# Attention spreads as turned columns, and the four layer norms moved from ScalarE to GpSimd

## The reference

```
h = relu(layernorm(x)); x = x + gat0(h, adj)     # one head:  Wh = h W^T; e = leaky(s1_i + s2_j); masked softmax; att @ Wh
h = relu(layernorm(x)); x = x + gat1(h, adj)     # four heads of 32 columns: the same with a bias, mask adj == 1
h = relu(layernorm(x)); x = x + sess(h, adj)     # sigmoid of leaky(h a_k h^T), chosen by adj == 1..4, times h, plus bias
h = relu(layernorm(x)); x = x + ggnn(h, adj)     # 3 GRU layers: m = A^T (h w); gi = m W_ih^T; gh = h W_hh^T; gates
```

## Time and profile before

| | |
|---|---|
| median of three runs | 1065.93 us (1064.18 to 1067.51) |
| the profiled execution's own time | 1066.04 us |
| its span, first to last instruction | 1063.9 us |
| granted TensorE clock, mean | 0.967 |
| PE (TensorE matmul) busy | 954.6 us, 90% |
| DVE (VectorE) busy | 892.3 us, 84% |
| ACT (ScalarE) busy | 864.0 us, 81% |
| POOL (GpSimd) busy | 132.6 us, 12% |

### The profile page before, as it was taken

One profiled execution on the slowest core, in us unless ns is written; L12 is line 12 of the kernel. 1 busy time (PEld: TensorE's weight loads), 2 busy tenths in 40 slices (PEclk: granted clock), 3 DMA queues, 4 the chain that ended last, 5 costly groups with the idle time before them and its releaser, 6 DMA issues.

```text
span 1063.9 us, 16086 instructions
## 1 busy us (share of the span) xinstructions
PE 954.6 (90%) x5024; PEld 609.6 (57%) x5024; DVE 892.3 (84%) x2710; ACT 864.0 (81%) x1860; POOL 132.6 (12%) x170
## 2 busy tenths in 40 slices
PE   4588998999989899999989899998989999998866
PEld 3455565666566566656556566656656665655443
DVE  5296989899898979899897989989897989979543
ACT  3367888979888897988888897988889798887742
POOL 1102011010202011020201201020201101010000
PEclk8558999999999999999999999999999999999989
DMA  2401204021210403121220402121030302111000
GB/s 72 109 1 39 72 11 109 11 61 52 68 51 14 106 11 77 44 60 51 56 64 10 110 11 60 60 61 51 15 105 11 79 31 61 50 40 51 1 11 10
DMA packets 42477, 52.32 MB, mean 49 GB/s; under 512 B 1296, under 2 KB 25872, under 8 KB 42384
## 3 DMA queue, kind: packets, MB, share of 16 engines
q0 software_dynamic: 16896, 25.17, 10.7%
q1 hardware_dynamic: 17040, 21.83, 6.5%
q10 hardware_dynamic: 8448, 4.20, 1.3%
HBM read 55.39 MB, written 4.19 MB: 56 GB/s over the span
## 4 chain that ended last, share of the span: by engine, by line
PE 52%; DVE 28%; ACT 10%; issue 6%; POOL 3%; DMA 0%; DVEq 0%; SPq 0%; ACTq 0%; POOLq 0%
PE l_bank L948 7%; DVE probs L642 6%; PE a_bank L981 6%; PE x_bank L1040 4%; PE a_bank L948 3%; PE h_bank L1102 3%; ACT hn L394 3%; PE r_bank L1102 3%; PE r_bank L1105 3%; DVE sess L843 3%; DVE sess L836 3%; PE h_bank L1105 3%; PE n_bank L1105 3%; DVE probs L663 3%; POOL rstd L363 2%
## 5 line engine op out<-in xcount | busy, mean ns | idle before, releaser
L663 DVE SCALAR_TENSOR_TENSOR probs<-spread,s_lift,probs 128x512 f32<-128x512 f32 x320 | 237.4, 747 | 4.0 <-DVE rmax L642 0.5
L642 DVE CUSTOM_DVE_ANT_0 probs<-spread,mask 128x512 f32<-128x512 f32 x320 | 211.8, 684 | 2.4 <-ACT spread L450 2.3
L363 POOL TENSOR_TENSOR rstd<-var_eps,power 128x4 f32<-128x4 f32 x64 | 88.0, 1375 | 882.5 <-DVE var_eps L636 603.0
L460 ACT ACTIVATE probs<-probs,shift_p 128x512 f32<-128x512 f32 x256 | 185.7, 725 | 5.7 <-DVE shift_p L659 5.7
L468 ACT ACTIVATE pT<-l_bank 128x512 f32<-128x512 f32 x256 | 151.8, 600 | 46.5 <-PE l_bank L948 46.3
L948 PEld LDWEIGHTS l_bank<-ident,probs 128*128 128x128 f32 x1024 | 124.3, 144 | 73.8 <-issue 46.0
L948 PE MATMUL l_bank<-ident,probs 128*128 128x128 f32 x1024 | 150.5, 278 | 6.1 <-ACT probs L460 5.1
L394 ACT ACTIVATE hn<-x,shift,rstd 128x128 f32<-128x128 f32 x192 | 80.5, 492 | 26.1 <-POOL shift L365 26.0
L1005 PE MATMUL l_bank<-hT,dst_rep 128*128 128x512 f32 x128 | 73.6, 658 | 12.1 <-ACT pT L468 8.5
L870 DVE SCALAR_TENSOR_TENSOR hid_n<-r_t,hid_n 128x512 f32<-128x512 f32 x48 | 33.1, 689 | 57.8 <-ACT r_t L518 57.8
L981 PE MATMUL a_bank<-values,pT 128*128 128x128 f32 x512 | 65.7, 286 | 0.7 <-ACT pT L428 0.7
(11 more groups left out here) (175 smaller groups left out, 1956.5 us busy)
## 6 DMA issues: line engine op xcount, KB each, us to landing
adjt_i<-in_adj_t SPq DMA_DIRECT2D x16, 1024.0 KB, 5.2
edges<-in_adj POOLq DMA_DIRECT2D x16, 1024.0 KB, 5.9
adj_h<-in_adj POOLq DMA_DIRECT2D x16, 512.0 KB, 7.7
xin<-in_x SPq DMA_DIRECT2D x16, 256.0 KB, 2.9
out<-out_sb ACTq DMA_DIRECT2D x16, 256.0 KB, 3.8
weights_sb<-in_weights SPq DMA_DIRECT2D x1, 840.0 KB, 4.7
```

What stands on the lines that cost most here:

```text
L363: g.tensor_tensor(rstd[n][:], var_eps[n][:], power[:], op=ALU.pow).then_inc(pool_step[n], 1)
L460: s.activation(row, row, ACT.Exp, bias=shift_p[:, head, c:c + 1], accum_out=den[:, head, c:c + 1]).then_inc(probs_ready, 1)
L642: return v.tensor_tensor_reduce(out=row, in0=spread_row, in1=mask, scale=1.0 / LIFT, scalar=-3e38, op0=ALU.subtract, op1=ALU.max, accum_ou ...
L663: v.scalar_tensor_tensor(row, spread_row, source, row, ALU.min, ALU.subtract, reverse1=True).then_inc(ready, 1)
```

## The change

Its parts, all in one step:

1. **Spreads.** `dst_rep` goes. The weights of the values get the source and target vectors as further columns (`values0_w` 130 wide, `values1_w` 136 wide), so one product of `hT` gives values, source and target numbers as columns. The spread of a head is then made by four transposes of its target column, read with a step of zero over 128 columns (`spread_column`), into the same bank. gat0's values no longer fit a bank, so three chunks go first and the last in a step of its own (`last0`), each with a ScalarE copy. `src0`, `s1_lift` and VectorE's L682 and L741 go; the two adds of gat1's values are 272 columns wide and take the constants along.
2. **Norms.** VectorE's minus the mean (L634) and GpSimd's multiply (L365) go. GpSimd makes `hn` without the ramp, four `tensor_scalar` of 128x128, (x - mean) times rstd. The ramp is taken by the copies that follow: `hT` by Relu in place of Copy, `state_hi` by Relu, `state_lo` by max(hn, 0) - state_hi. `hTa` is now read from `hT` instead of the bank, behind a wait for the copy of `hT`. For norm 2 the product with the rows needs the ramp too, so GpSimd takes it in place in one instruction of 128x512 behind TensorE's transposes (`ramp2`), and TensorE's w0 waits for it (`ramp_done`).
3. **Waits.** `turn_rows` waits for each chunk of `hn` instead of all four.
4. **Order.** New keys. In the steady part: values0 and last0 stand before dst0; values1 before x2, and x2 before g1_turn, on TensorE; values1 before scaled on VectorE; stats0, aggr0 and mean0 before g1_joint_r on VectorE. Between g0_agg and x2 (the next graph's) TensorE has the steps it had, less g1_turn and with values1; between scaled and mean3 VectorE has those it had, less values1 and src0. GpSimd: mean1 norm1_0..3 mean0 norm0_0..3 mean2 norm2_0..3 ramp2 edges values1 mean3 norm3_0..3.

```diff
+            def norm(p, n, c, rows):
+                if c == 0:
+                    pool.wait_ge(pool_step[n], p.count(1, 1))
+                    if p.before().exists():
+                        pool.wait_ge(hT_ready[n], p.before().count(1, 1))
+                g.tensor_scalar(hn[n][:, c, :], rows[:, c, :], moments[n][:, c, 0:1], rstd[n][:, c:c + 1],
+                                op0=ALU.subtract, op1=ALU.mult).then_inc(hn_ready[n], 1)
...
+                if step == "ramp2":
+                    pool.wait_ge(hT_ready[2], p.count(1, 1))
+                    g.tensor_scalar(hn[2][:, :, :], hn[2][:, :, :], 0.0, None, op0=ALU.max).then_inc(ramp_done, 1)
...
-                s.activation(hn[n][:, c, :], rows[:, c, :], ACT.Relu, bias=shift[n][:, c:c + 1],
-                             scale=rstd[n][:, c:c + 1]).then_inc(hn_ready[n], 1)
...
-                s.activation(hT[n][:, :], src[:, :], ACT.Copy).then_inc(hT_copied[n], 1)
+                s.activation(hT[n][:, :], src[:, :], ACT.Relu).then_inc(hT_copied[n], 1)
...
-                    s.activation(hTa[:, :], x_bank[:, :], ACT.Identity,
+                    act.wait_ge(hT_copied[2], p.count(1, 1))
+                    s.activation(hTa[:, :], hT[2][:, :], ACT.Identity,
...
-                v.tensor_scalar(minus_mean[n][:, :], moments[n][:, :, 0], -1.0, None, ALU.mult)
...
-                    for half in range(2):
-                        both = l_banks[half][:, 0:2 * (D + H1)].rearrange("p (c k) -> p c k", c=2)
-                        pair = slice(2 * half, 2 * half + 2)
-                        v.tensor_tensor(values1[:, pair, :], both[:, :, 0:D],
-                                        b1_rows[:, :].unsqueeze(1).to_broadcast([P, 2, D]), ALU.add)
-                        last = v.scalar_tensor_tensor(s1_lift[:, 1:HEADS, pair],
...
+                        both = l_banks[half][:, 0:2 * COLS1].rearrange("p (c k) -> p c k", c=2)
+                        v.tensor_tensor(values1[:, 2 * half:2 * half + 2, :], both,
+                                        b1_rows[:, :].unsqueeze(1).to_broadcast([P, 2, COLS1]),
+                                        ALU.add).then_inc(val1_copied, 1)
...
+            def spread_column(dst, columns, k, ready):
                 for c in range(C):
+                    last = t.transpose(dst[:, c * P:(c + 1) * P], columns[:, c, k:k + 1].to_broadcast([P, P]), ident[:])
+                last.then_inc(ready, 1)
...
+                    for c in range(C - 1):
+                        last = t.matmul(a_bank[:, c * COLS0:(c + 1) * COLS0], hT[0][:, c * P:(c + 1) * P],
+                                        values0_w[:, :], start=True, stop=True)
+                    last.then_inc(val0_ready, 1)
+                elif step == "last0":
+                    pe.wait_ge(val0_copied, p.count(1, 1))
+                    t.matmul(a_bank[:, 0:COLS0], hT[0][:, (C - 1) * P:], values0_w[:, :], start=True,
+                             stop=True).then_inc(last0_ready, 1)
...
-                    t.matmul(a_bank[:, :], dst_rep[:, 0, :], hT[0][:, :], start=True, stop=True).then_inc(dst0_ready, 1)
+                    pe.wait_ge(last0_copied, p.count(1, 1))
+                    spread_column(a_bank, values0, D + 1, dst0_ready)
...
-                    t.matmul(l_banks[head % 2][:, :], dst_rep[:, head, :], hT[1][:, :], start=True,
-                             stop=True).then_inc(dst_ready, 1)
+                    spread_column(l_banks[head % 2], values1, TARGET1 + head - 1, dst_ready)
...
+                        pe.wait_ge(ramp_done, p.count(1, 1))
```

More of the change, by code:

```diff
@@ L20 @@
 PLAIN = 1024.0
-A_STEPS = (["stats0", "aggr0", "mean0"] + [f"norm0_{c}" for c in range(4)] + ["rows0", "mask0", "dst0", "src0", "values0"] + [f"m{c}" for c in range(4)]
+A_STEPS = (["stats0", "aggr0", "mean0"] + [f"norm0_{c}" for c in range(4)] + ["rows0", "mask0", "values0", "last0", "dst0"] + [f"m{c}" for c in range(4)]
            + ["u0", "top0", "u1", "t0", "below0", "u2", "t1", "max0", "u3", "t2", "t3", "den0", "rden0"] + [f"sum0_{c}" for c in range(4)] + ["x1"])
-L_STEPS = (["stats1", "aggr1", "mean1"] + [f"norm1_{c}" for c in range(4)] + ["count", "rows1", "mask1", "dst1", "edges", "values1"]
+L_STEPS = (["stats1", "aggr1", "mean1"] + [f"norm1_{c}" for c in range(4)] + ["count", "rows1", "mask1", "edges", "values1", "dst1"]
            + [f"n{c}" for c in range(4)] + ["dst2"]
@@ L31 @@
 B_STEPS = ([f"sum1_{j}" for j in range(4)] + ["den1", "scaled", "x2", "stats2", "aggr2", "mean2"]
-           + [f"norm2_{c}" for c in range(4)] + ["rows2"] + [f"z{n}" for n in range(4)] + ["kinds"]
+           + [f"norm2_{c}" for c in range(4)] + ["rows2", "ramp2"] + [f"z{n}" for n in range(4)] + ["kinds"]
            + [f"s{n}" for n in range(4)] + [f"w{n}" for n in range(4)] + ["x3", "stats3", "aggr3", "mean3"]
@@ L280, in graph_layers @@
         pool_step = [sem(f"pool_step{n}") for n in range(NORMS)]
-        ln_ready = [sem(f"ln_ready{n}") for n in range(NORMS)]
         hn_ready = [sem(f"hn_ready{n}") for n in range(NORMS)]
@@ L381, in step_of @@
                     deviation(p, int(step[4]))
+                if step[:5] == "norm0":
+                    norm(p, 0, int(step[6]), xin[:, p.graph % 2, :, :])
+                if step[:5] == "norm1":
+                    norm(p, 1, int(step[6]), x1[:, p.graph % 2, :, :])
+                if step[:5] == "norm2":
+                    if step == "norm2_0" and p.before().exists():
+                        pool.wait_ge(av2_done, p.before().count(1, 1))
+                    norm(p, 2, int(step[6]), x2)
+                if step == "ramp2":
+                    pool.wait_ge(hT_ready[2], p.count(1, 1))
+                    g.tensor_scalar(hn[2][:, :, :], hn[2][:, :, :], 0.0, None, op0=ALU.max).then_inc(ramp_done, 1)
+                if step[:5] == "norm3":
+                    if step == "norm3_0" and p.before().exists():
+                        pool.wait_ge(rest_ready, p.before().count(LAYERS, 1))
+                    norm(p, 3, int(step[6]), x3)
             load_adj(Place(0))
@@ L389, in _ @@
             s = nc.scalar
-            def norm(p, n, c, rows):
-                if c == 0:
-                    act.wait_ge(ln_ready[n], p.count(1, 1))
-                s.activation(hn[n][:, c, :], rows[:, c, :], ACT.Relu, bias=shift[n][:, c:c + 1],
-                             scale=rstd[n][:, c:c + 1]).then_inc(hn_ready[n], 1)
             def copy_hT(p, n, src):
                 act.wait_ge(hT_ready[n], p.count(1, 1))
-                s.activation(hT[n][:, :], src[:, :], ACT.Copy).then_inc(hT_copied[n], 1)
+                s.activation(hT[n][:, :], src[:, :], ACT.Relu).then_inc(hT_copied[n], 1)
             def step_a(p, step):
                 prev = p.before()
-                if step[:5] == "norm0":
-                    norm(p, 0, int(step[6]), xin[:, p.graph % 2, :, :])
-                elif step == "rows0":
+                if step == "rows0":
                     copy_hT(p, 0, a_bank)
@@ L432, in step_l @@
                 prev = p.before()
-                if step[:5] == "norm1":
-                    norm(p, 1, int(step[6]), x1[:, p.graph % 2, :, :])
-                elif step == "rows1":
+                if step == "rows1":
                     copy_hT(p, 1, l_bank0)
@@ L476, in step_b @@
                     s.activation(avT[:, :], x_bank[:, :], ACT.Copy).then_inc(avT_copied, 1)
-                elif step[:5] == "norm2":
-                    if step == "norm2_0" and prev.exists():
-                        act.wait_ge(av2_done, prev.count(1, 1))
-                    norm(p, 2, int(step[6]), x2)
                 elif step == "rows2":
                     copy_hT(p, 2, x_bank)
-                    s.activation(hTa[:, :], x_bank[:, :], ACT.Identity,
+                    act.wait_ge(hT_copied[2], p.count(1, 1))
+                    s.activation(hTa[:, :], hT[2][:, :], ACT.Identity,
                                  scale=sess_sb[:, 0:1]).then_inc(hTa_ready, 1)
@@ L492, in step_b @@
                     s.activation(sess[:, j, :], sess[:, j, :], ACT.Tanh, scale=0.5).then_inc(tanh_ready, 1)
-                elif step[:5] == "norm3":
-                    if step == "norm3_0" and prev.exists():
-                        act.wait_ge(rest_ready, prev.count(LAYERS, 1))
-                    norm(p, 3, int(step[6]), x3)
                 elif step == "rows3":
@@ L507, in step_c @@
                         act.wait_ge(agg_ready, p.before().count(LAYERS, LAYERS))
-                    s.activation(state_hi[:, :, :], hn[3][:, :, :], ACT.Copy).then_inc(state_copied, 1)
+                    s.activation(state_hi[:, :, :], hn[3][:, :, :], ACT.Relu).then_inc(state_copied, 1)
                 elif step == "agg":
@@ L649, in shift_part @@
                     dve.wait_ge(max_ready[k], p.count(heads, nth))
-                    v.scalar_tensor_tensor(above[k][:, :], rmax[:, head, :], -1.0, s1_lift[:, head, :], ALU.mult, ALU.add)
```

(25 more changed lines are left out.)

116 lines of the change are left out of this document (52 added, 64 removed), and 120 rows, old and new, of the table WHEN.

## The result

The changed kernel takes 1211.83 us (median of 4 runs, 1210.55 to 1212.65), the kernel before 1065.06 us beside it (1063.36 to 1067.51). The ratio is 1.1375, with a 95% interval of 1.1348 to 1.1402: 147 us slower. The direction was forecast, the size was not: 1083 us, with 1120 as the upper end.

The account below looks back on a forecast made before the run. No engine was the bound, but a closed loop of GpSimd with ScalarE, TensorE, then VectorE. Per period +0.75 - 1.1 + 1.1 + 0.8 = +1.55 us, +22 over 14; 1066.0 + 22 - 5 = 1083 us, range 1042 to 1120.

Parts of the forecast that it names:

- The loop of three pieces: Closed loop in order: norm 3's power to g0_agg, 5.2 us; g0_agg to `scaled`, 30.9; `scaled` to norm 3's variance, 26.1.
- I take 0.29 alone, ends 0.20 and 0.49: Microseconds for one 128x128 norm operation on GpSimd without VectorE beside it, taken from an affine_select of the same shape.
- The hold on VectorE: Delay of VectorE by GpSimd's work beside it: 0.15 us for one norm, 0.5 for the ramp of 128x512.
- Rival 3: GpSimd holds VectorE for whole instructions, norm 2 late as well: period +5.65 us, 1140; half way about 1115; chance 0.21.
- It is worth nothing in the period: TensorE's spreads between x2 and g0_agg: some 3 us less work and 1.4 less waiting, but no gain per period.
- Rival 4: Spreads on TensorE: the transposed column costs as the matmul did, in the same slack; time stays 1083; no chance given.
- Their late end is covered ... only by about half a microsecond: Norm 2 and `ramp2`: TensorE reaches `rows2`, z0 and w0 after other steps, covering their late end by about 0.5 us.
- The forecast saving of 45: TensorE's busy time over the run was to fall by some 45 us.
- Norms 0 and 1 free: Norms 1 and 0 on GpSimd run in VectorE's slack, with over 4 us of cover, and cost nothing.
- ScalarE -100: ScalarE's busy time over the run was to fall by some 100 us.
- The order: From g0_agg to `scaled`: g1_turn leaves, values1 comes and its adds are partly covered, +0.75 us a period.
- The ends: Outside the repeated periods: about -4 us at the start, -1 at the last graph's norm 3, together -5.

Follow-up runs that it names:

- e5: Changed kernel with all norms back on ScalarE and the orders of the kernel before, leaving the turned spreads and waits by chunk: 1111.06 us, ratio 1.0442.
- e14: Kernel before, norms kept, with the spreads of gat1's heads 1 to 4 as turned columns, `values1` and `dst1` exchanging places on TensorE and ScalarE: 1098.10 us.
- e9: Kernel before, norms kept, with only the spreads of gat1's heads 2 to 4 as turned columns: 1070.33 us, ratio 1.0080.
- e4: Changed kernel with norm 2 alone back on ScalarE, without `ramp2`: 1166.52 us.
- e13: Changed kernel with matmuls that nobody reads added in TensorE's waits of `rows2` and `rows3`: 1174.60 us.
- e12: Kernel before with only norms 0 and 1 moved to GpSimd: 1065.63 us, ratio 1.0007.
- e7: Changed kernel, both spreads and norms changed, with the orders of the kernel before: 1182.74 us.
- e1: Changed kernel with all four norms back on ScalarE: 1128.19 us.
- e6: Kernel before with only the four norms moved to GpSimd and waits by chunk, its spreads and orders kept: 1156.43 us, ratio 1.0832.
- e11: Kernel before with the norms moved to GpSimd and its orders kept, norm 3 without its second operation (no multiply by rstd): 1134.37 us.
- e10: Kernel before with the norms moved to GpSimd and its orders kept, plus matmuls that nobody reads in the waits of `rows3`: 1128.43 us.

## Why the prediction was wrong

- **The loop of three pieces** was right, and carried the whole reading: forecast 5.2, 30.9, 26.1; measured 7.34, 32.84, 29.63. A period was to grow by 1.55 us and grew by 9.0.
- **"I take 0.29 alone, ends 0.20 and 0.49"** is the step that failed most. The price came from an instruction of the same shape but another kind. It is 0.78 alone, and 4.96 / 4 = 1.24 beside VectorE. Piece 1 grew by 2.95 us, not 0.8. The Trainium skill, "GPSIMD Engine Reference", section 3.1, has 1.03 cycles an element, an estimate of 0.11 us of streaming; the trace disagrees, since the shortest of 256 norms took 0.78.
- **The hold on VectorE** was about right: for a norm 0.15 was taken and 0.09 measured in the two rows above, for the ramp 0.5 was taken and 0.34 measured, though in two graphs only. Rival 3's whole-instruction hold did not happen, although its number (1115 to 1140) was the nearest. The rule of the Trainium skill that I weighed ("SBUF — State Buffer", "SBUF: two separate sides"), taken as one VectorE operation blocked for a whole GpSimd one, would have made it 0.78 for a norm; the rows above disagree.
- **"It is worth nothing in the period"**, of the spreads, failed: 45 us alone (e5). Head 1's first spread is 28 of them (e14 against e9), gat0's with the rest of part 1 another 13 (e5 against e14). I counted TensorE's time of a spread, which did lie in slack. I did not follow the new dependence, values before spread, to VectorE, whose piece of the loop was full, nor to ScalarE, which has norm 3 next in its order. Rival 4 had the same blind spot.
- **"Their late end is covered ... only by about half a microsecond"**, of norm 2: the cover was named and then trusted with the wrong length. With norms of 0.78 and more it was gone: norm 2 and its ramp cost 45 us (e4).
- **The granted clock** was in no term. I read 1.00 in the period and treated it as a constant. The waits that the change puts into `rows2` and `rows3` lower it, and at least 37 us hang on it (e13). That is also why TensorE's busy time rose by 42 us: in e13 it is 943 us without the added matmuls, 54 less than in the changed kernel. The forecast saving of 45 was too large even so: with the spreads alone (e5) TensorE is busy 936.3 us, 18 less than before.
- **Norms 0 and 1 free**: right (e12). **ScalarE -100**: 88.
- **The order**, +0.75 in piece 2: the new orders cost +0.9 there, and +1.0 in piece 3 that I did not see (e7 against changed).
- **The ends**, -5: they came to +15. The first power of norm 3 comes at 117.9 us with the norms on ScalarE (e1) and at 123.9 with only the norms moved (e6), so the longer norms eat the start's gain. The sixteenth graph pays as a period does: 62.16 us between the last two powers, against 51.74.

What stays open: how much of the new orders' 29 us is their places and how much is their mismatch with norms of this length; why the new orders cost 174 us with the old spreads; and what the waits by chunk do by themselves.

## What to carry to other kernels

Price a moved operation by an instruction of the same kind on the new engine, and where there is none, let the range reach several times past the nearest row; on a closed loop the price counts once per period. When a change makes a cheap step depend on a new one, follow the first use of its result, not its own time: three later spreads cost 5 us together, the first one of gat1 alone 28. And ask of every wait put on TensorE what the clock does behind it.

## What the runs showed of the hardware

- A float `tensor_scalar` of 128x128 with two per-partition scalars takes GpSimd 0.78 us, with one (e11) 0.59, ScalarE's activation of the same work 0.49. Beside a busy VectorE it is 1.24 us on average in norm 3.
- Where norm 3 runs beside VectorE, GpSimd's four instructions take 4.96 us instead of 3.13, and two of VectorE's last 0.09 us longer each: GpSimd bears nearly all of that contention. A GpSimd instruction of 128x512 costs VectorE more: 0.34 us on the logits that it meets (1.09 instead of 0.75).
- After waits of 1.76, 1.05, 0.38, 0.30 and 0.28 us with 0.3 to 0.5 us of work between them, TensorE's granted clock was 0.50 for 3.28 us and 0.86 for the next 3.50. With matmuls in the waits of this place it was 1.00 in 15 graphs of 16 (e10), and in 8 of 16 in the changed kernel (e13).
